# A fused grouped convolution, base layer and routed LoRA kernel on one core: the first loads cut smaller and put in another order, one low part moved to GpSimd, and y_lo taken last by TensorE

## What is computed

```python
# cond: convolution along the 512 positions (9 taps, 4 groups), condition, bias
out = lax.conv_general_dilated(x, weight, (1,), [(4, 4)], feature_group_count=4)
h = out + einsum('nd,od->no', c, c_weight)[:, :, None] + bias[None, :, None]
# ffn on h, 128*32 rows of 512
base_out = einsum('btd,od->bto', h, base_W) + base_b
probs = softmax(einsum('btd,nd->btn', h, router_W) + router_b)   # 15 routes
topk_p, topk_i = top_k(probs, 8)
w = sum of topk_p by expert_map[topk_i]                          # 8 experts
lora = einsum('bter,eor->bto', einsum('btd,erd->bter', h, A) * w[..., None], B) * 2
return x + base_out + lora
```

## Time and profile before

| | us |
|---|---|
| three runs | 187.00, 186.97, 185.57 |
| median | 186.97 |
| profiled execution | 185.48 |
| its span, first to last instruction | 183.7 |
| PE busy in it | 179.3 |

### The profile page before, as it was taken

The page is one execution under the profiler, slowest core; times in us unless marked ns, Lnnn a source line. Parts: engine busy times, 40 slices in busy tenths (PEclk is TensorE's granted clock), DMA queues, the critical chain, the costliest instruction groups (busy, mean ns, idle before and its releaser), DMA issues.

```text
span 183.7 us, 3924 instructions
## 1 busy us (share of the span) xinstructions
PE 179.3 (98%) x1234; PEld 170.6 (93%) x1234; DVE 150.5 (82%) x509; ACT 81.1 (44%) x247; POOL 140.6 (77%) x139
## 2 busy tenths in 40 slices
PE   7999999999999999999999999999999999999993
PEld 2587999999999999999999999999999999999992
DVE  0588879888888988888898888888898889878574
ACT  3748734354543435454443545444344544422320
POOL 2427999987888988798899888888988887895410
PEclk9999999999999999999999999999999999999999
DMA  5999752736575453546465354756545721333304
GB/s 193 386 319 332 266 173 67 237 124 208 171 228 171 157 177 116 197 161 228 122 220 195 110 184 152 228 177 192 173 108 171 262 88 52 106 114 114 118 0 171
DMA packets 17588, 32.01 MB, mean 174 GB/s; under 512 B 1952, under 2 KB 2720, under 8 KB 17568
## 3 DMA queue, kind: packets, MB, share of 16 engines
q1 hardware_dynamic: 17136, 31.27, 52.3%
q10 hardware_dynamic: 432, 0.49, 0.8%
HBM read 23.36 MB, written 8.39 MB: 173 GB/s over the span
## 4 chain that ended last, share of the span: by engine, by line
PE 83%; POOL 8%; DVE 4%; issue 2%; ACT 1%; DVEq 0%; ACTq 0%; POOLq 0%
PE wide_ps L604 53%; PE wide_ps L644 11%; PE conv_banks L590 10%; POOL xr L476 3%; PE edge_bank L590 2%; POOL y_lo L499 2%; PE conv_banks L604 2%; PE wide_ps L550 2%; PE odd_bank L631 2%; POOL terms_lo L481 2%; DVE wide_lo L222 1%; DVE y L849 1%; POOL conv_lo L470 1%; DVE xr L966 1%; DVE y_rows L764 1%
## 5 line engine op out<-in xcount | busy, mean ns | idle before, releaser
L604 PE MATMUL wide_ps<-wide_hi,y_hi 128*128 128x400 f32 (+1 forms) x248 | 79.2, 326 | 0.3
L604 PE MATMUL wide_ps<-wide_hi,y_lo 128*128 128x400 f32 (+1 forms) x248 | 76.0, 314 | 0.0
L604 PE MATMUL wide_ps<-wide_lo,y_hi 128*128 128x400 f32 (+1 forms) x248 | 75.2, 312 | 0.0
L481 POOL TENSOR_TENSOR terms_lo<-terms,terms_hi 128x512 fp32r<-128x512 f32 x28 | 36.3, 1296 | 18.8 <-ACT terms_hi L377 18.8
L604 PEld LDWEIGHTS wide_ps<-wide_hi,y_hi 128*128 128x128 f32 x248 | 46.3, 188 | 2.7 <-issue 1.1
L604 PEld LDWEIGHTS wide_ps<-wide_lo,y_hi 128*128 128x128 f32 x248 | 46.5, 188 | 0.0
L604 PEld LDWEIGHTS wide_ps<-wide_hi,y_lo 128*128 128x128 f32 x248 | 46.3, 188 | 0.1
L476 POOL TENSOR_TENSOR xr<-xr,base_b_sb 128x512 f32<-128x512 f32 x32 | 41.5, 1298 | 3.6 <-DMA xr<-x_rows 3.6
L499 POOL TENSOR_TENSOR y_lo<-y,y_hi 128x512 fp32r<-128x512 f32 x30 | 38.8, 1295 | 2.0 <-ACT y_hi L392 2.0
L399 ACT ACTIVATE hw_hi<-odd_bank 128x128 fp32r<-128x128 f32 x31 | 8.6, 278 | 54.9 <-PE odd_bank L631 54.9
L758 DVE TENSOR_TENSOR xr<-wide_ps,xr 128x512 f32<-128x512 f32 x30 | 20.7, 691 | 5.0 <-PE wide_ps L644 3.5
(11 more groups left out here) (89 smaller groups left out, 309.3 us busy)
## 6 DMA issues: line engine op xcount, KB each, us to landing
xr<-x_rows SPq DMA_DIRECT2D x32, 256.0 KB, 3.7
out<-xr SPq DMA_DIRECT2D x31, 256.0 KB, 3.2
terms<-x_units SPq DMA_DIRECT2D x28, 256.0 KB, 2.9
edges<-x_edges SPq DMA_DIRECT2D x14, 256.0 KB, 3.2
wide_sb<-wide_w SPq DMA_DIRECT2D x4, 328.0 KB, 4.3
x_in<-x_first SPq DMA_DIRECT2D x4, 264.0 KB, 4.1
weights_sb<-conv_w SPq DMA_DIRECT2D x2, 192.0 KB, 4.9
weights_sb<-conv_w SPq DMA_DIRECT2D x1, 256.0 KB, 4.2
```

The source lines that it names most:

```text
L481: nc.gpsimd.tensor_tensor(terms_lo[i % 2][:, :, :, :], terms[i][:, :, :, :], terms_hi[i % 2][:, :, :, :].bitcast(F32), ALU.subtract)\
L604: mm = nc.tensor.matmul(sums_of(t, k)[:, b, 0:columns[1] - columns[0]], a[k % 2][:, r, :], w[:, r, columns[0]:columns[1]], start=r == 0 an ...
```

## The change

The first loads are cut and ordered anew: tile 0 of x comes in two halves of 8 sequences each with a semaphore for each; the condition's inputs and the first two convolution matrices, one load before, are two loads of ACT's queue, the matrices first; the next two matrices move from ACT's queue to SP's. PE convolves tile 0 in two halves of 256 columns. WARM_UP goes from 8 to 6. wide_lo of slice 0 goes from POOL to DVE, y_lo of tile 1 from DVE to POOL. cond_sums of groups 2 and 3 go ahead of the last two slices' W_REST. From step 3 on, POOL makes y_lo ahead of the biased rows, and PE takes the front products by kind in all steps but the last two. In step 2 DVE turns tile 4 ahead of hw_low.

```diff
-WARM_UP = 8
+WARM_UP = 6
...
-W_PIECES = (slice(0, COND + 2 * P), slice(COND + 2 * P, COND + 4 * P),
+W_PIECES = (slice(COND, COND + 2 * P), slice(COND + 2 * P, COND + 4 * P),
...
+            def load_first_x(n, rows):
+                sync.dma_start(x_in[0][:, rows, :], x_first[0][:, rows, :])\
+                    .then_inc(x_first_in[n], 16)
...
-            load_x(0)
+            for n, rows in enumerate(FIRST_ROWS):
+                load_first_x(n, rows)
+            load_conv(1)
+            load_x(1)
             load_wide(0)
-            load_x(1)
             load_wide(1)
-            sync.wait_ge(x_loaded[0], 16)
+            sync.wait_ge(x_first_in[1], 16)
             load_wide(2)
             load_wide(3)
-            sync.wait_ge(wide_in[0], 16)
+            sync.wait_ge(x_loaded[1], 16)
             load_conv(2)
             load_x(2)
-            sync.wait_ge(wide_in[1], 16)
+            sync.wait_ge(wide_in[0], 16)
             load_conv(3)
             load_x(3)
-            sync.wait_ge(wide_in[3], 16)
+            sync.wait_ge(wide_in[2], 16)
             load_terms(START, 0)
             load_edges(START // 2, 0)
...
-            for piece in range(2):
+            def load_conv(piece):
                 own = W_PIECES[piece]
                 act.dma_start(weights_sb[:, own], conv_w[:, own]).then_inc(conv_w_in[piece], 16)
+
+            load_conv(0)
+            act.dma_start(cond_in_sb, conv_w[:, 0:COND]).then_inc(cond_in, 16)
...
-            act.wait_ge(conv_w_in[0], 16)
+            act.wait_ge(cond_in, 16)
             cond_weights(slice(0, 1))
             cond_weights(slice(1, GROUPS))
-            wide_high(range(1))
             bias_condition(range(1), 1)
             conv_high(0)
-            wide_high(range(1, RUNS))
+            wide_high(range(RUNS))
             bias_condition(range(1, 2), 2)
...
-            pool.wait_ge(wide_hi_ready, 1)
-            wide_low_part(nc.gpsimd, 0, wide_lo_first)
...
             conv_low(0)
             conv_low(1)
 
-            pool.wait_ge(y_lo_first, 2)
+            y_low(1, 1, 2)
             edge(START // 2, 0)
...
-                    y_low(t + 2, k + 2, 3)
+                    y_low(t + 2, k + 2)
...
+                if from_tile(t, 3) and up_to_tile(t, TILES - 2):
+                    y_low(t + 1, k + 1)
                 if up_to_tile(t, TILES - 1):
                     bias_rows(t, k)
-                if from_tile(t, 3) and up_to_tile(t, TILES - 2):
-                    y_low(t + 1, k + 1)
...
-                if t == 0:
-                    cond_sums(range(1), 1)
...
+                if groups.start == 0:
+                    pe.wait_ge(cond_in, 16)
...
-            for t in range(2):
-                pe.wait_ge(conv_w_in[t], 16)
-                pe.wait_ge(x_loaded[t], 16)
-                conv_first(t)
+            pe.wait_ge(conv_w_in[0], 16)
+            for n, rows in enumerate(FIRST_ROWS):
+                pe.wait_ge(x_first_in[n], 16)
+                for j, block in ((W_OWN[0], 0), (W_REACH[0], 1)):
+                    if n == 1 and block == 1:
+                        cond_sums(range(1), 1)
+                    mm = nc.tensor.matmul(first_ps[:, 0, rows, :], conv_sb[:, j, :],
+                                          x_in[0][:, rows, block:block + BLK],
+                                          start=j == W_OWN[0], stop=j == W_REACH[0])
+            mm.then_inc(conv_done, 1)
+            pe.wait_ge(conv_w_in[1], 16)
+            pe.wait_ge(x_loaded[1], 16)
+            conv_first(1)
...
-                pe.wait_ge(wide_lo_first, 1)
-                linear(0, 0, (0,), products=(W_REST,))
-                pe.wait_ge(wide_lo_ready, 1)
-                linear(0, 0, (1,), products=(W_REST,))
-                pe.wait_ge(wide_lo_ready, RUNS - 1)
+                for r in runs[:RUNS // 2]:
+                    pe.wait_ge(wide_lo_ready, r + 1)
+                    linear(0, 0, (r,), products=(W_REST,))
+
+                cond_sums(range(2, GROUPS), 2)
+                pe.wait_ge(wide_lo_ready, RUNS)
                 for bank, done in ((FRONT_BANK, front_done), (NEXT_BANK, linear_done)):
                     linear(0, 0, runs[RUNS // 2:], (bank,), (W_REST,), (RUNS - 1, W_REST))\
                         .then_inc(done, 1)
-                cond_sums(range(2, GROUPS), 2)
                 conv_later(2)
...
-                pe.wait_ge(y_lo_first, 2)
+                pe.wait_ge(y_lo_ready, 2)
...
                     pe.wait_ge(out_added, t - 1)
-                    if t == 2:
-                        pe.wait_ge(y_hi_ready, t + 1)
-                        linear(t, k, runs, (FRONT_BANK,), (HIGH,))
-                        linear(t, k, runs, (FRONT_BANK,), (W_REST,))
-                        pe.wait_ge(y_lo_ready, t + 1)
-                        linear(t, k, runs, (FRONT_BANK,), (Y_REST,)).then_inc(front_done, 1)
-                    else:
-                        pe.wait_ge(y_lo_ready, t + 1)
-                        linear(t, k, runs, (FRONT_BANK,)).then_inc(front_done, 1)
+
+                    pe.wait_ge(y_hi_ready, t + 1)
+                    linear(t, k, runs, (FRONT_BANK,), (HIGH,))
+                    linear(t, k, runs, (FRONT_BANK,), (W_REST,))
+                    pe.wait_ge(y_lo_ready, t + 1)
+                    linear(t, k, runs, (FRONT_BANK,), (Y_REST,)).then_inc(front_done, 1)
...
-                if t < 4:
-
-                    if t == 3:
-                        dve.wait_ge(y_hi_ready, t - 1)
-                else:
+
+                if from_tile(t, 3):
                     dve.wait_ge(y_lo_ready, t - 1)
...
-                wide_low_part(nc.vector, r, wide_lo_ready)
+                nc.vector.tensor_tensor(wide_lo[:, r, :], wide_sb[:, r, :],
+                                        wide_hi[:, r, :].bitcast(F32), ALU.subtract)\
+                    .then_inc(wide_lo_ready, 1)
...
-            wide_low(1)
-            wide_low(2)
-            wide_low(3)
+            for r in range(RUNS):
+                wide_low(r)
             dve.wait_ge(cond_biased, 2)
             condition_first(1)
             turn(1, 1)
             choose(0, 0)
             dve.wait_ge(logits_ready, 1)
             best(0, 0)
-            y_low(1, 1)
...
-                    if t > 2:
-                        turn(t + 2, k + 2)
+                    turn(t + 2, k + 2)
                     hw_low(t - 1, k - 1)
-                    if t == 2:
-
-                        turn(t + 2, k + 2)
```

More of the change, by code:

```diff
@@ L31 @@
 START = 4
+FIRST_ROWS = (slice(0, Q // 2), slice(Q // 2, Q))
 RUNS = BP // 4
@@ L145, in build @@
         conv_w_in = [sem(f"conv_w_in{i}") for i in range(len(W_PIECES))]
+        cond_in = sem("cond_in")
         cond_w_ready = sem("cond_w_ready")
@@ L152, in build @@
         conv_lo_ready = sem("conv_lo_ready")
+        x_first_in = [sem(f"x_first_in{i}") for i in range(2)]
         x_loaded = [sem(f"x_loaded{i}") for i in range(START)]
@@ L156, in build @@
         wide_hi_ready = sem("wide_hi_ready")
-        wide_lo_first = sem("wide_lo_first")
         wide_lo_ready = sem("wide_lo_ready")
@@ L219, in up_to_tile @@
             return t <= most
-        def wide_low_part(ops, r, ready):
-            ops.tensor_tensor(wide_lo[:, r, :], wide_sb[:, r, :], wide_hi[:, r, :].bitcast(F32),
-                              ALU.subtract).then_inc(ready, 1)
         def sums_of(t, k):
@@ L863, in wide_low @@
                 dve.wait_ge(wide_hi_ready, r + 1)
-                wide_low_part(nc.vector, r, wide_lo_ready)
+                nc.vector.tensor_tensor(wide_lo[:, r, :], wide_sb[:, r, :],
+                                        wide_hi[:, r, :].bitcast(F32), ALU.subtract)\
+                    .then_inc(wide_lo_ready, 1)
             def y_low(t, k):
-                if t > 0:
-                    dve.wait_ge(y_hi_ready, t + 1)
-                else:
-                    dve.wait_ge(y_hi_first, 1)
+                dve.wait_ge(y_hi_first, 1)
                 nc.vector.tensor_tensor(y_lo[k % 2][:, :, :], y[k % 2][:, :, :],
@@ L873, in y_low @@
                     .then_inc(y_lo_first, 1)
-            dve.wait_ge(conv_w_in[0], 16)
+            dve.wait_ge(cond_in, 16)
             dve.wait_ge(index_ready, E)
```

## The result

| | before | after |
|---|---|---|
| median of 18 executions, us | 185.92 | 184.85 |
| shortest, longest | 185.29, 187.00 | 184.02, 185.33 |
| profiled execution | 185.48 | 184.44 |
| its span | 183.7 | 182.6 |

The ratio of the times is 0.9927, with a 95% interval of 0.9907 to 0.9946, which is 1.35 us of the median before; the two medians differ by 1.07. Five of the 18 executions before lie apart at 186.8 to 187.0 (mean 186.91), the other 13 have a mean of 185.71, and the 18 after a mean of 184.82. So against the lower group, a split made with the times in view, the change is worth 0.90 us, and the rest comes from the upper group, which has no counterpart after.

What follows compares the result with a forecast made beforehand. PE, busy without gaps from 33.2 us, was taken as the bound, so only earlier waits count. Terms -0.37 + 0.16 - 0.70 = -0.91 us, taken from the median 186.97, gave 186.1 us, range 184.3 to 187.3.

Steps and rivals of the forecast that it cites:

- The rival that put the same sum on the lower level: Whole kernel: same -0.91 us, but the median falls on the lower level of executions, 184.6 us; chance 0.27.
- Part 1: First convolution: smaller first loads let PE start at 3.7 us instead of 4.44; gain 0.37 us, bounds 0 and 0.5.
- Part 2: From y_hi to the end of tile 0's products: DVE's added fourth wide_lo costs 0.16 us, bounds 0 and 0.4.
- Part 3: y_lo of tile 1 on POOL: 1.3 us there against 0.7 on DVE, hidden with 0.6 to spare.
- Part 4: PE's three late starts at 27.09, 30.80 and 33.21 us all go: gain 0.70 us, bounds 0.2 and 0.75.
- (c): Tile 4's front products at 33.21 us, waiting for POOL's y_lo of tile 4: 0.37 us to gain.
- (a): First front matmul at 27.09 us, restarting after a wait for add_out: 0.09 us to gain.
- (b): Last third of up in step 2, at 30.80 us, waiting for hw_low: 0.24 us to gain.
- Part 5: Steady steps: POOL's swapped order and PE's order by kind cost 0; bounds -0.1 and 0.3 for 27 steps.
- Rival (3): Startup: the shorter warm-up keeps PE's clock at 1.2 GHz longer; +0.55 us, 186.0 or 187.5 by level; chance 0.10.
- Rival (4): Whole kernel: start hides more of the slow clock, DVE's head start carries further; -1.5 us, 185.5; chance 0.08.

Runs made afterwards that it cites:

- e4: Kernel before with only tile 4's turn put ahead of hw_low in step 2: 185.88 us, ratio 1.0007.
- e12: Changed kernel with y_lo of tile 1 back on VectorE (DVE) from POOL: 184.71 us, ratio 0.9946.
- e1: Changed kernel with the old order of front products, of POOL's y_lo and biased rows, and of tile 4's turn, leaving the new start: 186.67 us, ratio 1.0031.
- e2: Kernel before with only the steps' three edits (front by kind, y_lo ahead of biased rows, tile 4's turn ahead of hw_low): 184.95 us, ratio 0.9953.
- e3: Kernel before with only the front products by kind from step 3 on: 185.57 us, ratio 0.9987.
- e5: Kernel before with only POOL's y_lo ahead of the biased rows from step 3 on: 185.26 us, ratio 0.9992.
- e6: Kernel before with no zero matmuls (WARM_UP 0 for 8): 187.84, 187.92, 187.98 and 188.06 us in four executions, ratio 1.0111.
- e11: Kernel before with GpSimd's second conv_lo held back until VectorE has made its three wide_lo: 186.28 us, ratio 1.0016.
- e7: Changed kernel with 3 zero matmuls in place of 6: 186.47 us, ratio 1.0014.
- e9: Changed kernel with the first wide weights loaded ahead of tile 1 of x on SP's queue: 185.07 us, ratio 0.9955.
- e8: Changed kernel with 8 zero matmuls in place of 6: 185.54 us, ratio 0.9973.
- e10: Changed kernel with GpSimd's second conv_lo held back until VectorE has made all four wide_lo: 185.24 us, ratio 0.9956.

## Why the prediction was right, and where it was not

The sum was -0.91 against the profiled execution's own time; the two profiles differ by 1.04, the lower group of before and the executions after by 0.90. The single number, 186.1, was 1.25 too high, because of the step behind the sum: "for the median I take the level of the median". Three executions with two on the upper level gave a median of 186.97, and 18 gave 185.92, with 5 on that level. The rival that put the same sum on the lower level said 184.6. That 184.85 lies within 184.3 to 187.3 is owed to a range that took in both levels, and not to the choice between them. The sum's nearness is in part luck as well: up to the turn of tile 4 the profile gains 0.81 where 0.91 was counted, and the 0.27 behind it was counted as nothing.

- **Part 1.** Start 3.7, measured 3.64: right. The landing came as the rate of ACT's queue had it (0.13 MB had gone by 3.0 us, 3.2 counted), and not by the two-part cost of the Trainium skill (DMA: Bandwidth & Descriptors, on the two cost components), from which I had estimated 4.2; that section fits DMAs issued by GpSimd, and these are ACT's and SP's. Tile 1's convolution started at 6.24 and not at 6.10. The clock was misread: I took 0.10 us in the first record for half speed and put the step at 4.64. e4, whose records are all at full pace, has 0.08 of it too, so it is the first record's fill; in the profile of before the step came by 4.5 or so, in the one after near 4.8. Of the 0.80 that PE starts sooner, 0.55 is given back at half pace, the longer fill included, and 0.25 arrives. Gain 0.37 counted, 0.25 measured.
- **Part 2.** The assumption "what comes behind them lands as before" was wrong: wide_hi waited 0.59 for its first weights and started at 7.27, and PE waited 0.16 for the fourth. It cost nothing more, since the fourth wide_lo sets the end there. It ends at 12.13 (near 12.0 counted), and PE takes up W_REST at 12.23 (12.03 counted). Loss 0.16 counted, 0.13 measured. Of the two parts 0.12 is left at tile 1, not 0.21.
- **Part 3.** Hidden, with 0.44 to spare for the 0.6 counted. POOL's first edges began 1.07 later (15.60 for 14.53), beyond the bound of 0.9, and what stands behind them 0.55 to 0.65. The cause was only half seen: the tile's late rows, counted in part 2, reach POOL through ACT's terms_hi, and that weighs more than the y_lo itself (about 0.5 and 0.16). e12 shows that the y_lo costs nothing here, and e1 what the whole start costs without the cover: 0.69.
- **Part 4.** 0.68 measured and 0.69 in e2, for 0.70. The places are those named; e3 to e5 show (c) cleared by either of the two orders, and (a) and (b) by the turn (e4's thirds of up are 0.24 apart), with (b)'s gain lost again at (c).
- **Part 5.** "Cost 0" with bounds of -0.1 and 0.3 missed on the good side: 0.27 less. From the turn of tile 4 to that of tile 31 the eight profiles with front by kind gain 0.22 to 0.36 on the kernel before; the other five, with front slice by slice, gain 0.14 and 0.29 (e1, e4) and lose 0.03, 0.07 and 0.09 (e6, e11, e5). The means differ by 0.23, some 0.01 a tile, but e4 lies in the middle of the other group, and each is one profile. Whether the order by kind is a little quicker stays open.
- **Rival (3)** was real as a mechanism (e7: 186.47) but not with the 6 zeros of the change.
- **Rival (4)** had a grain of truth: the upper group is gone in the 18 executions after. That a late step lies under long executions is shown in the profiles and by e6. The profiles also say what one costs in either kernel: e5's, with the old start and the step at 6.3, has the turn of tile 0 1.43 late, 0.50 of it for the collision, and 185.48 + 1.43 is 186.9, where the upper group lies (an estimate); e9's, with the new start and the step at 6.5, has it 0.88 later than the profile after, and took 185.31, which is within the range after. So the change may meet late steps as often and pay less for them. That it does is not shown: no profile of the changed kernel itself has a late step, e8's, with the new start and 8 zeros, has the collision, and e1, with the new start and the wait for y_lo of tile 4, has 7 of 12 between 186.65 and 187.36. Of the 53 executions of the changed kernel, e9, e10 and e12 only one (185.96) lies apart. This stays open.

## What to carry to other kernels

An edit that makes a helper engine later and an edit that lets the main engine ask later belong together: alone the first lost 0.3% and the second gave 0.5%, together they gave 0.7%. What makes the helper later need not be the work moved to it: here most came from another engine's longer list, through a third. Waits in series hide each other: two edits each cleared the same wait (0.33 and 0.37 in the profiles), the third gave 0.01 alone, and the three 0.69, while the medians of each alone didn't differ from before. And where a program of some 190 us starts with a TensorE at 1.2 GHz, a median of three tells the moment of the clock's step as much as the kernel: read it from the pace of the first records before a level is chosen.

## What the runs showed of the hardware

- The step to 2.4 GHz came between 4.4 and 7.0 us in profiles of one and the same beginning, near 7.8 without zero matmuls and near 8.0 with three of them and an idle time behind. A us of delay costs about half a us in the turn of tile 0 as long as nothing else is met (new start, step at 4.8, 5.3, 6.5, 8.0: -0.12, +0.16, +0.76, +1.38), while the granted clock of the profile says 1.00 throughout.
- A VectorE subtraction of 128x656 from two SBUF tiles took 1.52 us beside a GpSimd subtraction of the same kind, and 0.84 otherwise. The Trainium skill (SBUF — State Buffer, on the shared port pair) says that a VectorE instruction with two SBUF inputs and a GpSimd one that reads SBUF hold a port pair exclusively, for the whole instruction, and the other blocks. The rows agree: in e2, e3, e5, e6 and e8 alike the wide_lo that met a conv_lo ended 0.70 after that conv_lo had (e8: 13.64 and 12.94), as if it did its work only then. The delay is 0.68 where GpSimd's instruction takes 0.86, because that one was already under way; in e7 it was GpSimd that lost, 1.48 for 0.86, and ended 0.73 behind the wide_lo.
- The first record of the first convolution takes 0.08 to 0.16 us more than its pace in thirteen of fourteen profiles, which is easily read as a slow clock.
